# First loads, slot set-up, last stores and the written order of all five engine programs changed in a one-core attention and slot-memory kernel

## The reference

```python
x = x + attn(layernorm(x))
x = x + slots(layernorm(x))
# attn: q = tanh(x Wc + bc); shell = x Ws + bs, normalised; proj = shell omega^T + bias
# phi = ([1, q, q^2, q^3, q^4] scaled) outer [cos(proj), sin(proj)] @ W_combine^T
# softmax(causal(phi phi^T * decay(|i-j|) / temp)) @ (x Wv + bv) @ Wout + bout
# slots: h = gelu([x, mean slot] w1 + b1); top 8 of 64 of (h w2 + b2)/tau -> softmax = alpha
# slot_input = alpha^T x / sum(alpha); one GRU step on the slots; out = alpha (slots wv + bv) wo + bo
```

## Time and profile before

| | |
|---|---|
| median of 3 runs | 743.97 us |
| the profiled execution | 743.47 us |
| its span, first to last instruction | 741.6 us |
| mean granted TensorE clock | 0.997 |
| TensorE matmul busy | 718.1 us, 97% |
| DVE, ACT, POOL busy | 583.9, 426.1, 403.2 us |

### The profile page before, as it was taken

One profiled execution on the slowest core, in us unless ns is written; L12 is line 12 of the kernel. 1 busy time (PEld: TensorE's weight loads), 2 busy tenths in 40 slices (PEclk: granted clock), 3 DMA queues, 4 the chain that ended last, 5 costly groups with the idle time before them and its releaser, 6 DMA issues.

```text
span 741.6 us, 14845 instructions
## 1 busy us (share of the span) xinstructions
PE 718.1 (97%) x4576; PEld 550.3 (74%) x4576; DVE 583.9 (79%) x1802; ACT 426.1 (57%) x841; POOL 403.2 (54%) x857
## 2 busy tenths in 40 slices
PE   8989999999899999999999999999999999999996
PEld 4867777686696877778697777779687777866765
DVE  5769687686878888888878888887888889876753
ACT  4448484936456584655648575555658465556341
POOL 6655757362665646375565647466464637544510
PEclk9999999999999999999999999999999999999998
DMA  8171120202232140323223031322314032121103
GB/s 283 37 223 32 32 58 1 57 26 89 59 102 70 51 114 10 113 58 114 58 86 88 30 106 38 113 59 95 77 47 116 11 115 58 58 57 59 43 15 114
DMA packets 49397, 55.09 MB, mean 74 GB/s; under 512 B 5990, under 2 KB 40360, under 8 KB 49320
## 3 DMA queue, kind: packets, MB, share of 16 engines
q1 hardware_dynamic: 48114, 53.48, 25.5%
q10 hardware_dynamic: 1206, 0.67, 0.4%
HBM read 20.58 MB, written 16.78 MB: 50 GB/s over the span
## 4 chain that ended last, share of the span: by engine, by line
PE 82%; POOL 4%; issue 4%; DMA 3%; ACT 3%; DVE 3%; SPq 0%; POOLq 0%; DVEq 0%; ACTq 0%
PE ps L234 16%; PE ps L260 16%; PE ps L345 15%; PE ps L371 7%; PE ps L316 6%; PE ps L420 6%; PE ps L295 4%; PE ps L484 4%; PE ps L405 4%; POOL Z L1222 3%; DMA xmT<-Z 2%; PE ps L383 2%; PE ps L297 2%; PE ps L464 2%; ACT xn L606 1%
## 5 line engine op out<-in xcount | busy, mean ns | idle before, releaser
L345 PE MATMUL ps<-VS,ET 128*128 128x257 f32 x640 | 153.9, 380 | 0.0
L1222 POOL TENSOR_TENSOR Z<-Z,QB 128x512 f32<-128x512 f32 x64 | 81.5, 1274 | 109.6 <-ACT Z L648 107.7
L345 PEld LDWEIGHTS ps<-VS,ET 128*128 128x128 f32 x640 | 114.9, 189 | 14.4 <-issue 1.3
L606 ACT ACTIVATE xn<-X,rs 128x256 f32<-128x256 f32 x128 | 66.3, 593 | 75.3 <-POOL rs L1161 75.3
L667 ACT ACTIVATE ET<-ps 128x128 f32<-128x128 f32 (+3 forms) x128 | 55.8, 438 | 83.1 <-PE ps L234 81.0
L657 ACT ACTIVATE E<-ps,nmax 128x128 f32<-128x128 f32 (+3 forms) x128 | 64.8, 528 | 50.6 <-DVE nmax L868 48.2
L260 PE MATMUL ps<-W1h,xh 128*128 128x354 f32 x256 | 87.6, 342 | 2.9 <-DVE VS L799 1.5
L799 DVE TENSOR_TENSOR VS<-ps,biasM 128x354 f32<-128x354 f32 x128 | 66.2, 521 | 26.4 <-PE ps L260 24.8
L260 PE MATMUL ps<-W1l,xh 128*128 128x354 f32 x256 | 83.0, 324 | 0.0
L260 PE MATMUL ps<-W1h,xl 128*128 128x354 f32 x256 | 82.3, 322 | 0.0
L1193 POOL TENSOR_SCALAR xm<-X,rs 128x256 f32<-128x256 f32 x128 | 71.5, 572 | 1.1 <-POOL rs L1182 1.1
...
## 6 DMA issues: line engine op xcount, KB each, us to landing
X<-in_x SPq DMA_DIRECT2D x32, 512.0 KB, 4.3
xmT<-Z SPq DMA_DIRECT2D x128, 128.0 KB, 2.3
out_x<-X SPq DMA_DIRECT2D x32, 512.0 KB, 3.6
...
```

Of the source, the lines that this page charges most:

```text
L345: ins = e.matmul(p[:, 0:D + 1], ET[:, r % 2, j * 128:j * 128 + 128], VS[:, (2 * k + d) % 4, j, 0:D + 1], start=j == 0, stop=j == i)
L606: ins = e.activation(xn[:, d, t, :], X[:, b % NX, t, :], ACT.Identity, bias=rs[:, d, 2, t:t + 1], scale=rs[:, d, 1, t:t + 1])
L1222: e.tensor_tensor(Z[:, i + 1, :], Z[:, i, :], QB[:, :], ALU.mult).then_inc(s["zm"], 1)
```

## The change

- ACT's queue keeps W_v and W_outT and the biases; W_shell, omegaT and W_scT go to SP's queue behind `load_x(0)` (`weight_loads`). `load_x(1)` now waits until all five have landed; `load_x(2)` goes ahead of `first_loads`.
- `slot_setup` on TensorE is cut in two; `warm(14)` in it is gone, and `warm(6)` and `warm(11)` stand ahead of it. Other `warm` counts in the end are changed.
- The last pair's two sequences are stored in four halves instead of two wholes.
- All five lists are in another order: prologue, loop and end. In the loop the step set is the same; some steps move over the loop's boundary.

```diff
@@ TensorE: set-up, prologue's start, loop, end
-                warm(14)
+            def gates_setup():
                 e.wait_ge(s["slot_evac"], 1)
...
-            weights_setup(); xn_t(0, 0, 0); xn_t(0, 0, 1); bias_setup(); xn_t(0, 1, 0); xn_t(0, 1, 1)
-            proj(0, 0, 0); proj(0, 0, 1); proj(0, 0, 2); proj(0, 0, 3); proj(0, 1, 0); proj(0, 1, 1)
-            proj(0, 1, 2); proj(0, 1, 3); xn_t(1, 0, 0); xn_t(1, 0, 1); q_t(0); slot_setup(); z_t(0)
-            proj(1, 0, 0); proj(1, 0, 1); xn_t(1, 1, 0); proj(1, 0, 2); proj(1, 0, 3); xn_t(1, 1, 1); phi(0)
-            proj(1, 1, 0); logits(0, 0); proj(1, 1, 1); proj(1, 1, 2); xn_t(2, 0, 0); e_t(0, 0); e_t(0, 1)
-            logits(0, 1); values(0, 0); proj(1, 1, 3); e_t(0, 2); values(0, 1); e_t(0, 3); logits(0, 2)
+            weights_setup(); xn_t(0, 0, 0); xn_t(0, 0, 1); bias_setup(); proj(0, 0, 0); xn_t(0, 1, 0)
+            xn_t(0, 1, 1); proj(0, 0, 1); proj(0, 0, 2); proj(0, 0, 3); proj(0, 1, 0); proj(0, 1, 1)
+            proj(0, 1, 2); proj(0, 1, 3)
+            warm(6)
+            q_t(0); xn_t(1, 0, 0); xn_t(1, 0, 1)
+            warm(11)
+            slot_setup(); gates_setup()
+            z_t(0); xn_t(1, 1, 0); xn_t(1, 1, 1); proj(1, 0, 0); proj(1, 0, 1); proj(1, 0, 2); proj(1, 0, 3)
+            proj(1, 1, 0); proj(1, 1, 1); proj(1, 1, 2); proj(1, 1, 3); phi(0); q_t(1); logits(0, 0)
+            e_t(0, 0); e_t(0, 1); logits(0, 1); e_t(0, 2); values(0, 0); values(0, 1); e_t(0, 3); e_t(0, 4)
...
             for it in range(3, NP - 1):
-                xn_t(p, 0, 0); xn_t(p, 0, 1); e_t(n, 0); gx_rz(m); proj(p, 0, 0); proj(p, 0, 1)
-                xn_t(p, 1, 0); e_t(n, 1); gx_n(m); logits(n, 1); out_mm(g, 1); al_t(m); xn_t(p, 1, 1)
-                proj(p, 0, 2); proj(p, 0, 3); proj(p, 1, 0); proj(p, 1, 1); proj(p, 1, 2); proj(p, 1, 3)
-                values(n, 0); e_t(n, 2); xm_t(f, 0, 0); xm_t(f, 0, 1); values(n, 1); values(n, 2); e_t(n, 3)
-                xm_t(f, 1, 0); xm_t(f, 1, 1); hidden(f, 0); hidden(f, 1); q_t(p); values(n, 3); route(f)
-                logits(n, 2); e_t(n, 4); z_t(p); rt_t(f); e_t(n, 5); values(n, 4); values(n, 5); e_t(n, 6)
-                slot_v(m); e_t(n, 7); values(n, 6); values(n, 7); phi(p); gather(f); logits(p, 0)
-                out_mm(m, 0); gi_t(f)
+                gather(m); logits(n, 0); out_mm(g, 0); gi_t(m); xn_t(p, 0, 0); xn_t(p, 0, 1); e_t(n, 0)
+                gx_rz(m); proj(p, 0, 0); proj(p, 0, 1); proj(p, 0, 2); proj(p, 0, 3); e_t(n, 1)
+                values(n, 0); e_t(n, 2); gx_n(m); xn_t(p, 1, 0); xn_t(p, 1, 1); out_mm(g, 1); logits(n, 1)
+                xm_t(f, 0, 0); proj(p, 1, 0); proj(p, 1, 1); proj(p, 1, 2); proj(p, 1, 3); values(n, 1)
+                xm_t(f, 0, 1); xm_t(f, 1, 0); values(n, 2); xm_t(f, 1, 1); e_t(n, 3); hidden(f, 0)
+                hidden(f, 1); e_t(n, 4); q_t(p); values(n, 3); route(f); logits(n, 2); e_t(n, 5); z_t(p)
+                rt_t(f); values(n, 4); values(n, 5); e_t(n, 6); e_t(n, 7); slot_v(m); values(n, 6); al_t(m)
+                values(n, 7); phi(p)
             x, y, z = NP - 3, NP - 2, NP - 1
-            out_mm(x, 1); gx_n(y); xm_t(z, 0, 0); xm_t(z, 0, 1); gx_rz(y); hidden(z, 0); xm_t(z, 1, 0)
-            xm_t(z, 1, 1)
+            gather(y); out_mm(x, 0); gi_t(y); gx_rz(y); out_mm(x, 1); xm_t(z, 0, 0); xm_t(z, 0, 1); gx_n(y)
+            al_t(y); hidden(z, 0); xm_t(z, 1, 0); xm_t(z, 1, 1)
             e.wait_ge(s["E"], 8 * NP)
-            warm(6)
-            hidden(z, 1); slot_v(y); route(z); al_t(y); rt_t(z); out_mm(y, 0)
+            warm(4)
+            hidden(z, 1)
+            warm(4)
+            route(z); slot_v(y); rt_t(z)
+            out_mm(y, 0)
             warm(20)
@@ ACT: queue, first steps, loop
-            load(wsh, a["W_shell"], "wa")
-            load(omT, a["omegaT"], "wa")
-            load(W1[:, :, 257:322], chunks(a["W_scT"]), "wa")
...
-            ln_norm(0, 0); ln_norm(0, 1); xn_high(0, 0, 0); xn_high(0, 0, 1)
+            ln_norm(0, 0); xn_high(0, 0, 0); xn_high(0, 0, 1); ln_norm(0, 1); xn_high(0, 1, 0)
+            xn_high(0, 1, 1)
...
-                rz_tanh(m); al_copy(m); xn_high(p, 1, 1); probs_t(n, 2); xm_copy(f, 0, 0); xm_copy(f, 0, 1)
-                n_tanh(m); charge(p); expo(n, 4); xm_copy(f, 1, 0); xm_copy(f, 1, 1); probs_t(n, 3)
-                expo(n, 5); gelu(f, 0); gelu(f, 1); q_copy(p); sine(p); rt_out(f); probs_t(n, 4); z_copy(p)
-                probs_t(n, 5); expo(n, 6); expo(n, 7); route_exp(f, 0); probs_t(n, 6); probs_t(n, 7)
-                route_exp(f, 1)
+                xn_high(p, 1, 0); xn_high(p, 1, 1); probs_t(n, 2); xm_copy(f, 0, 0); charge(p)
+                xm_copy(f, 0, 1); expo(n, 4); xm_copy(f, 1, 0); xm_copy(f, 1, 1); n_tanh(m); expo(n, 5)
+                probs_t(n, 3); gelu(f, 0); gelu(f, 1); q_copy(p); probs_t(n, 4); sine(p); rt_out(f)
+                probs_t(n, 5); z_copy(p); expo(n, 6); expo(n, 7); probs_t(n, 6); route_exp(f, 0)
+                probs_t(n, 7); route_exp(f, 1); al_copy(m)
@@ DVE: first steps, part of the loop
-            ln_stats(0, 0, 0); ln_stats(0, 0, 1); ln_stats(0, 1, 0); ln_stats(0, 1, 1); weights_setup()
+            ln_stats(0, 0, 0); ln_stats(0, 0, 1); ln_stats(0, 1, 0); ln_stats(0, 1, 1); ln_stats(1, 0, 0)
+            ln_stats(1, 0, 1); weights_setup(); xn_low(0, 0, 0); xn_low(0, 0, 1); bias_setup(); vs(0, 0, 0)
...
+                attended(f, 6); lm_stats(f, 6); attended(f, 7); lm_stats(f, 7); qk_full(n)
+                ln_stats(p, 1, 0); gathered(m); row_max(n, 0); row_max(n, 1); row_max(n, 2); finish(g, 0, 0)
@@ POOL: first steps
-            ln_scale(0, 0); ln_scale(0, 1); columns(); attention_setup(); ln_scale(1, 0); square(0, 0)
-            slot_setup(); square(0, 1); rnorm(0); ln_scale(1, 1); power(0, 0); power(0, 1); power(0, 2)
+            columns(); ln_scale(0, 0); ln_scale(0, 1); ln_scale(1, 0); attention_setup(); square(0, 0)
+            square(0, 1); rnorm(0); slot_setup(); ln_scale(1, 1); power(0, 0); power(0, 1); power(0, 2)
@@ SP
+                if b == 1:
+                    e.wait_ge(s["wa"], 16 * 5)
...
+                if k == NP - 1:
+                    for z in range(2):
+                        e.wait_ge(s["fin"], 4 * k + 2 * d + z + 1)
+                        e.dma_start(out[2 * k + z].rearrange("(t p) d -> p t d", p=128)[:, 2 * d:2 * d + 2, :],
+                                    X[:, (2 * k + z) % NX, 2 * d:2 * d + 2, :]).then_inc(s[f"st{(2 * k + z) % NX}"], 16)
+                    return
...
-            load_x(0); load_x(1); first_loads(); load_x(2); load_x(3); slot_loads(); load_x(4); z_moves(0)
+            load_x(0); weight_loads(); load_x(1); load_x(2); first_loads(); load_x(3); slot_loads()
+            load_x(4); load_x(5); z_moves(0); load_x(6); load_x(7); z_moves(1); load_x(8); z_moves(2)
...
-                load_x(2 * it + 4); store(o, 1); load_x(2 * it + 5); z_moves(n); store(g, 0)
+                store(o, 1); load_x(2 * it + 4); z_moves(n); load_x(2 * it + 5); store(g, 0)
```

More of the change, by code:

```diff
@@ L542, in _ @@
-            e_t(1, 2); values(1, 0); xm_t(0, 0, 1); logits(1, 1); xn_t(3, 0, 1); values(1, 1); hidden(0, 0)
-            logits(1, 2); xm_t(0, 1, 0); xm_t(0, 1, 1); e_t(1, 3); values(1, 2); q_t(2); e_t(1, 4)
-            hidden(0, 1); xn_t(3, 1, 0); values(1, 3); e_t(1, 5); values(1, 4); route(0); e_t(1, 6); z_t(2)
-            xn_t(3, 1, 1); values(1, 5); rt_t(0); values(1, 6); e_t(1, 7); proj(3, 0, 0); proj(3, 0, 1)
-            values(1, 7); phi(2); proj(3, 0, 2); proj(3, 0, 3); logits(2, 0); xm_t(1, 0, 0); proj(3, 1, 0)
@@ L547, in _ @@
-            proj(3, 1, 1); e_t(2, 0); xm_t(1, 0, 1); proj(3, 1, 2); proj(3, 1, 3); e_t(2, 1); e_t(2, 2)
-            values(2, 0); xn_t(4, 0, 0); xn_t(4, 0, 1); hidden(1, 0); gather(0); logits(2, 1); values(2, 1)
-            e_t(2, 3); xm_t(1, 1, 0); gi_t(0); values(2, 2); e_t(2, 4); q_t(3); xm_t(1, 1, 1); values(2, 3)
-            e_t(2, 5); hidden(1, 1); logits(2, 2); z_t(3); gx_rz(0); values(2, 4); al_t(0); values(2, 5)
-            xn_t(4, 1, 0); route(1); gx_n(0); e_t(2, 6); xn_t(4, 1, 1); rt_t(1); phi(3); values(2, 6)
@@ L552, in _ @@
-            slot_v(0); proj(4, 0, 0); proj(4, 0, 1); e_t(2, 7); logits(3, 0); out_mm(0, 0); proj(4, 0, 2)
-            values(2, 7); e_t(3, 0); proj(4, 0, 3); values(3, 0); e_t(3, 1); xm_t(2, 0, 0); proj(4, 1, 0)
-            out_mm(0, 1); logits(3, 1); xm_t(2, 0, 1); proj(4, 1, 1); proj(4, 1, 2); proj(4, 1, 3)
-            e_t(3, 2); e_t(3, 3); xm_t(2, 1, 0); values(3, 1); gather(1); logits(3, 2); al_t(1)
-            hidden(2, 0); gi_t(1); xm_t(2, 1, 1); q_t(4); values(3, 2); hidden(2, 1); e_t(3, 4); gx_rz(1)
@@ L557, in _ @@
-            gx_n(1); route(2); e_t(3, 5); rt_t(2); values(3, 3); values(3, 4); z_t(4); e_t(3, 6)
-            values(3, 5); slot_v(1); e_t(3, 7); values(3, 6); values(3, 7); phi(4); gather(2); logits(4, 0)
-            out_mm(1, 0); gi_t(2)
```

(20 more changed lines are left out.)

226 lines of the change are left out of this document (115 added, 111 removed).

## The result

The changed kernel takes **746.26 us** (median of 8 runs, 744.73 to 748.91) against 743.58 for the kernel before, run beside it: ratio 1.0041, 95% interval 1.0021 to 1.0061. It is a little slower; the prediction said 736.8, and 733.6 to 741.8. The profiled execution is at 746.66 with a span of 744.9.

A forecast was written before the change was run, and what follows sets the result against it. TensorE, busy 97% of the span, was taken as the bound, so only its waits, fillers and the ends could give time. Gains 1.7 + 1.3 + 1.8 + 1.4 + 1.0 = 7.2 us gave 736.8 us, range 733.6 to 741.8.

The forecast's parts named there:

- Set-up and fill to phi(1): First loads through phi(1): earlier weights and projections gain 1.7 us; bounds a loss of 2 and a gain of 3.5.
- rival D: Loop: load_x(2it+5) behind the z moves lands too late for ln_stats(p, 1, 0); slower, 748.9 us; chance 0.07.
- the sum of waits behind phi(0): Between phi(0) and phi(1): TensorE's waits in pair 0's attention chain, added up to 4.9 us.
- Rest of the prologue: phi(1) to phi(4): three fewer activation table loads on ACT end several waits; gain 1.3 us, bounds nothing and 3.5.
- The loop: Per iteration, e_t(n, 6)'s 0.23 us wait for expo 6 goes, 12 times; gain 1.8 us after a deduction, at most 2.8.
- z moves and tight places: Loop: a us deducted from the 2.8 us gain for waits on z moves and steps with little time to spare.
- The end: Last pair's tail: n_tanh(14) done before xm_copy(15, 1, 0), earlier rt_t and shift(15, 1); gain 1.4 us, 0.8 to 2.2.
- The stores: Behind the last finish: halves leave 256 KB in place of 512 per sequence; gain 1.0 us, 0.4 to 1.6.
- The fit that I took from the Trainium skill: Last stores: a transfer costs 2.0 us plus bytes at 436 GB/s, so a half saves 0.6 us.
- Rival B: First loads: weights land at 10.05 as before, x(1) and x(2) later, TensorE idles; 740.5 us; chance 0.07.

The follow-up runs named there:

- fill_head: Changed kernel with 17 filler matmuls where TensorE idles ahead of the fourth weight product; 742.35 us, ratio 0.9971 to the kernel before.
- final: early_filled with DVE's weight copies right behind x(0)'s statistics, TensorE's head reordered, 10 fillers for 17, slot_values(13) heading DVE's tail; 734.98 us, ratio 0.9868.
- early_filled: Changed kernel with loads_early and fill_head together, plus more fillers at the idle moments around phi(0); 737.33 us, ratio 0.9922.
- loads_early: Changed kernel with x(4) and x(5) each loaded as soon as its own slot is free, ahead of the z moves; 742.29 us, ratio 0.9976.
- final_old_loads: final with the five weights back on ACT's queue and no wait ahead of x(1); 743.40 us, ratio 0.9982.
- old_loads: early_filled with the five weights back on ACT's queue and no wait ahead of x(1); 738.51 us, ratio 0.9935.

## Why the prediction was wrong, point by point

**Set-up and fill to phi(1), forecast 1.7 us of gain, and a loss of 2 at most: this is the step that failed.** The measured sum to phi(1) is 85.9 us for my 73.6. Against the 75.3 of the kernel before with the same work done, the gain of 1.7 is a loss of 10.6. Three things in it were wrong.

*The clock.* I wrote of the first 20 us and the loop that "none of this is a matter of the clock". That was read from a kernel whose fillers kept TensorE busy, and says nothing of one that idles 3.9 us. Fillers alone, which bring no work forward, gave back some 5 us. Nor did I see the idle time coming: my estimate had the copies at 13.4 and asked only when the first projection could start, not what TensorE does until then. With the products issued at 8.6 and three banks, it stands from 11.

*The landings.* I had the weights landed at 6.4 (x(1) was issued at 7.35), x(1) at 10.7 (its statistics start at 11.25) and the copies at 13.4 (14.54). Half a us to one us each, all on the late side. Of the 3.5 us by which the first projection missed (21.28 for 17.8), fillers alone gave back 1.9 (19.39 in fill_head).

*The z moves.* Of the slot set-up I wrote that "it ends near 39.8 either way, which hides the 17 fillers that replace 14": it ended at 46.1, as it hangs on pair 0's projections, which end 5.5 us later than before. With those on time it does end there: z moves start at 41.36 in final, at 41.18 before. And phi(0) by the earlier trace rows "came 7.1 us after their start", which I kept for the new queue order, although the change puts x(5) ahead of the moves. I followed load_x(2it+5) in the loop (rival D) and not load_x(5) in the prologue. early_filled and final have 25.2 us from phi(0) to phi(1), my figure, and loads_early has 25.5. So the sum of waits behind phi(0) was about right at full clock; the first two have fillers in those waits. But even final, with everything repaired and a better order on DVE, reaches phi(1) only at 75.45: nothing of the 1.7 is gained.

**Rest of the prologue, 1.3:** too small. The 119.1 forecast were 116.81, a gain of 3.6, just past my upper bound of 3.5. The 116.5 to 118.0 us of the experiments make it 2.4 to 3.9. No run splits it between the table loads and the other waits.

**The loop, 1.8:** 2.67 between phi(4) and phi(15), 11 x 0.24. Period and place are as predicted, and the earlier table load is there as the cause, though no run tried it by itself. The us that I took off for z moves and tight places was not needed (from 196 to 620 us TensorE waits 0.6 for z moves and 0.2 for DVE).

**The end, 1.4:** wrong in sign. From the last phi to the last finish it is 0.4 slower. I followed gx_rz(14) and n_tanh(14) and missed that slot_values(13) now stands behind six steps on DVE while gather(14) comes first on TensorE and needs its bank: 1.6 us. Nor did n_tanh(14) clear the way as I said: it runs at 711.10, and xm_copy(15, 1, 0) starts at 712.40, 45.6 us behind phi(15), where it was 44.9. With slot_values(13) moved the end gains 1.2, near the forecast.

**The stores, 1.0:** 1.5 by two pairs of profiles, near the upper bound of 1.6. The fit that I took from the Trainium skill (DMA: Bandwidth & Descriptors, Anatomy of one DMA) is given there for transfers that GpSimd issues; these stores are SyncE's, and the 0.6 us by it was too small.

**Rival B,** that the weights would be no sooner, was wrong: SP's wait for the weights ended by 7.35, where TensorE had waited for them until 10.05. Of the Trainium skill's rule (DMA: Bandwidth & Descriptors, Rules for kernel authors) the half on bandwidth agrees: 233 GB/s in the first 20 us after and 286 before, so no gain; but what a queue sheds also lets the small transfers behind it land sooner, here by 3.6 us (final against final_old_loads) and 4.6 (early_filled against old_loads). No rival held the mechanism that decided. D has the right sign by luck: its place in the loop is fine.

With both losses repaired, the head of DVE's list rearranged, the tail's step moved and fillers added, the change gives 734.98 us, 1.3% below before, near the span that I forecast (733.5 for 734.4). That the sums agree is in part luck: up to phi(1) final gains nothing where I had 1.7, from there to phi(4) 2.6 for 1.3, on to phi(15) 2.8 for 1.7, to the last finish 1.2 for 1.4, and behind it 1.6 for 1.0.
